# A fourth bank for the ring of exact scores, taken from the output of the heads

## What is computed

```python
x = ln(x + splat_attention(x))            # 16 heads of 16
x = ln(x + cross_attention(x, ctx))       # 16 heads of 16, 120 keys
x = ln(x + best_of_8_experts(x))
x = ln(x + causal_attention(x))           # 16 heads of 16
x = ln(x + two_blocks(x, ctx))            # self, then cross: 16 heads of 32, each with an MLP 256-1024-256
x = ln(x + four_of_16_experts(x))
# an attention, for every head:
p = exp(q @ k.T * scale - max)            # later divided by its row sum
o = p @ v                                 # v has a column of ones: the row sum comes along
```

## Time and profile before

| | us |
|---|---|
| median of 3 runs | 3960.23 |
| lowest, highest | 3958.79, 3975.51 |
| the profiled execution | 3954.29 |
| its span, first to last instruction | 3952.6 |
| PE busy | 3343.7 |
| DVE busy | 2807.9 |
| ACT busy | 2094.5 |
| POOL busy | 975.9 |

### The profile page before, as it was taken

One profiled execution on the slowest core, in us unless ns is written; L12 is line 12 of the kernel. 1 busy time (PEld: TensorE's weight loads), 2 busy tenths in 40 slices (PEclk: granted clock), 3 DMA queues, 4 the chain that ended last, 5 costly groups with the idle time before them and its releaser, 6 DMA issues. The chain is left out here.

```text
span 3952.6 us, 94629 instructions
## 1 busy us (share of the span) xinstructions
PE 3343.7 (85%) x38960; PEld 2374.8 (60%) x38960; DVE 2807.9 (71%) x6362; ACT 2094.5 (53%) x4222; POOL 975.9 (25%) x1808
## 2 busy tenths in 40 slices
PE   1889888989898888888988888899888898988886
PEld 1666565666565656656656656566655665655554
DVE  5777776777776767777776667677776677777664
ACT  4745565455556554564564555645555556455551
POOL 0312341122222321131132222212342112124310
PEclk9989888988898889888988988898988898989887
DMA  5000000000000000000000000000000000000000
GB/s 163 3 3 2 2 3 4 9 7 3 2 2 2 8 3 7 7 3 2 7 2 2 5 4 7 6 4 2 1 2 3 9 9 4 2 2 2 1 4 6
DMA packets 30365, 31.49 MB, mean 8 GB/s; under 512 B 8673, under 2 KB 26482, under 8 KB 29938
## 3 DMA queue, kind: packets, MB, share of 16 engines
q1 hardware_dynamic: 29938, 25.44, 2.1%
HBM read 21.24 MB, written 4.19 MB: 6 GB/s over the span
## 5 line engine op out<-in xcount | busy, mean ns | idle before, releaser
L1103 ACT ACTIVATE p<-bank,p_log 128x512 f32<-128x512 f32 (+2 forms) x1280 | 746.8, 583 | 1331.3 <-PE bank L797 1266.6
L1669 POOL TENSOR_TENSOR prob<-p,prob 120x256 f16<-120x256 f32 (+2 forms) x512 | 455.5, 890 | 1742.4 <-ACT prob L1104 1741.3
L1104 ACT ACTIVATE prob<-bank,p_log 128x512 f16<-128x512 f32 (+2 forms) x1280 | 747.3, 584 | 0.0
L1368 DVE TENSOR_REDUCE negm<-bank 128x2 f16<-128x512 f32 (+1 forms) x1280 | 675.3, 569 | 33.9 <-PE bank L752 18.2
L1286 DVE TENSOR_TENSOR prob<-p,prob 128x512 f16<-128x512 f32 (+2 forms) x768 | 474.0, 624 | 188.9 <-ACT prob L1104 178.8
L774 PE MATMUL bank<-q,k 32*128 32x256 f16 (+2 forms) x6144 | 496.8, 289 | 65.1 <-issue 34.7
L668 PE MATMUL bank<-w_exp,ident_h 128*128 128x512 f16 x1280 | 429.3, 421 | 32.3 <-DVE negm L1368 15.2
L1678 POOL TENSOR_SCALAR_AFFINE_SELECT probm<-prob 128x128 f16<-128x128 f16 x1024 | 325.9, 358 | 340.4 <-DVE prob L1286 340.4
L774 PEld LDWEIGHTS bank<-q,k 32*128 32x128 f16 (+1 forms) x6144 | 307.9, 110 | 142.7 <-issue 66.8
L797 PE MATMUL bank<-ident_h,negm 128*128 128x256 f16 (+2 forms) x2560 | 384.9, 273 | 0.0
L1661 POOL TENSOR_TENSOR rstd<-veps,minus_half 128x2 f32<-128x2 f32 (+1 forms) x208 | 149.7, 720 | 887.9 <-DVE veps L1261 887.3
(11 more groups left out here) (300 smaller groups left out, 6286.5 us busy)
## 6 DMA issues: line engine op xcount, KB each, us to landing
x<-in_x SPq DMA_DIRECT2D x16, 256.0 KB, 2.7
out<-z SPq DMA_DIRECT2D x16, 256.0 KB, 2.2
xa<-in_li SPq DMA_DIRECT2D x9, 256.0 KB, 4.6
x<-in_li SPq DMA_DIRECT2D x7, 256.0 KB, 4.3
z<-in_wq SPq DMA_DIRECT2D x4, 256.0 KB, 4.4
z<-in_li SPq DMA_DIRECT2D x4, 256.0 KB, 4.1
cx<-in_ctx_t SPq DMA_DIRECT2D x16, 60.0 KB, 1.8
cx<-in_ctx SPq DMA_DIRECT2D x16, 60.0 KB, 1.8
```

Of the source, the lines that this page charges most:

```text
L1103: act(p32[0:n, g % PBUF32, 0:cols], ps[0:n, 0:cols], ACT.Exp, bias=p_log[0:n, :], scale=a.scale)
L1104: act(prob[0:n, 0, g % PBUF, 0:cols], ps[0:n, 0:cols], ACT.Exp, bias=p_log[0:n, :], scale=a.scale).then_inc(a_done, one(a_done))
L1368: v.tensor_reduce(negm[:, h * NT:(h + 1) * NT], ring_v[bank_of(e, v_full)][:, :].rearrange("p (t n) -> p t n", t=NT)[:, :, 0:ATTNS[k].keys ...
L1669: g.tensor_tensor(prob[0:n, 1, m % PBUF, 0:cols], p32[0:n, m % PBUF32, 0:cols], prob[0:n, 0, m % PBUF, 0:cols], ALU.subtract).then_inc(pp_ ...
```

## The change

`RING` becomes three numbers: `ring_a` has four banks (0 to 3), `ring_v` three (4 to 6), `o_bank` one (7). A use of `ring_a` now waits for the use four before it. A group of heads waits for the normalisation of the group just before it, since both use bank 7.

```diff
-RING = 3
+RING_A, RING_V, RING_O = 4, 3, 1
...
-        ring_a, ring_v, o_bank = bank[0:3], bank[3:6], bank[6:8]
+        ring_a, ring_v, o_bank = bank[0:RING_A], bank[RING_A:RING_A + RING_V], bank[8 - RING_O:8]
...
                     taken = releases[which]
-                    if len(taken) >= RING:
-                        e.wait_ge(*taken[-RING])
+                    ring = ring_a if which == "a" else ring_v
+                    if len(taken) >= len(ring):
+                        e.wait_ge(*taken[-len(ring)])
...
-                    return (ring_a if which == "a" else ring_v)[(len(taken) - 1) % RING]
+                    return ring[(len(taken) - 1) % len(ring)]
...
                     group = sent(o_full)
-                    if h % a.group == 0 and group >= 2:
-                        e.wait_ge(o_done, group - 1)
+                    if h % a.group == 0 and group >= RING_O:
+                        e.wait_ge(o_done, group + 1 - RING_O)
...
-                        o = o_bank[group % 2][:, c:c + D + 1]
+                        o = o_bank[group % RING_O][:, c:c + D + 1]
...
-                    o = o_bank[(sent(o_done)) % 2][:, :].rearrange("p (t c) -> p t c", t=NT)[:, :, 0:n * (D + 1)]
+                    o = o_bank[sent(o_done) % RING_O][:, :].rearrange("p (t c) -> p t c", t=NT)[:, :, 0:n * (D + 1)]
```

More of the change, by code:

```diff
@@ L91, in __init__ @@
     def __init__(self):
-        self.increments, self.awaited = {}, {}
+        self.increments, self.awaited, self.ring = {}, {}, {}
     def one(self, sem):
@@ L109, in bank_of @@
     def bank_of(self, engine, full):
-        return (self.awaited[(str(engine.engine), full.num)] - 1) % RING
+        return (self.awaited[(str(engine.engine), full.num)] - 1) % self.ring[full.num]
 def heads_of(a):
@@ L386, in decoder @@
         counts = Counts()
+        counts.ring.update({a_full.num: RING_A, v_full.num: RING_V})
         one, sent, upcoming, bank_of = counts.one, counts.sent, counts.upcoming, counts.bank_of
@@ L631, in slot @@
                         ready[what] = taken[-1]
-                        low_banks.append((len(taken) - 1) % RING)
+                        low_banks.append((len(taken) - 1) % len(ring))
                         high[what] = high_ready, len(low_banks)
-                    return (ring_a if which == "a" else ring_v)[(len(taken) - 1) % RING]
+                    return ring[(len(taken) - 1) % len(ring)]
                 def to_raw(*what):
@@ L832, in weighted_values @@
                             for pp, vp in PARTS:
-                                last = mm(o_bank[group % 2][:, c:c + D], probm[:, pp, g % MBUF, i, :],
+                                last = mm(o_bank[group % RING_O][:, c:c + D], probm[:, pp, g % MBUF, i, :],
                                           val[s][:, vp, i * HEADS + h, 0:D], start=False,
```

## The result

The changed kernel takes 4025.59 us (median of 4 runs, 4021.61 to 4030.78), against 3961.95 us of the kernel before beside it. The ratio is 1.0155, 95% interval [1.0128, 1.0181]: it is slower by 1.6%. The forecast was 4100 us, 3.5% slower.

The account below looks back on a forecast made before the run. The prediction took PE to set the end, its idle time being what could move. From 3954.3 us, less 36 for the ring, plus 122 for new waits and 58 for the clock, it got 4098, named 4100; range 4042 to 4160.

Parts of the forecast that it names:

- What bounds the kernel: Whole kernel: PE sets the end, busy 3343.7 of 3952.6 us; its 609 us of idle time is what can move.
- The new wait: At PE's changes of head group: 158.5 us of waiting for DVE's normalisation, 118 inside pairs, 38 at heads 13 to 14.
- What of it reaches the end: Behind the 61 waiting places: 122 us comes through, nine tenths of that inside pairs, 37% at heads 13 to 14.
- the clock: PE's granted clock after idles above 2 us: 22 more low stretches at 2.6 us each cost 58 us.
- The ring's gain: At PE's waits for ring_a: a fourth bank gains 36 us, a little over half of five waits totalling 64.6 us.
- The signs named for the profile: Changed profile: o_tok waits 130 to 160 us, ring_a waits nearly gone, two others down 20 to 40, PE busy up 30 to 60.
- The ring wins: Rival, stages between attentions: ring_a waits vanish and the clock falls less, 3890 us; chance of faster 0.03.
- The banks do not bind: Rival, ring_a: the fourth bank gives nothing, since a pair takes two at once; 4134 us, no chance of its own.
- the waits are absorbed: Rival, PE's waits on DVE: a third of 158.5 us passes, 3971 us; chance 0.05 shared with no-change rival, partly absorbed 0.09.
- The clock costs more: Rival, PE's clock: each of 38 long waits starts a 10 us low stretch, 4178 us; chance above 4160 is 0.13.
- Rotation does not matter: Rival, o_bank: only DVE's emptying is exposed, 29 us of new waits, 3947 us; chance 0.05 shared with absorbed waits.

Follow-up runs that it names:

- the waits alone: Kernel before, banks unchanged, but each group of heads waits for the normalisation of the group just before it, as with one output bank: 4111.53 us, ratio 1.0361.
- even groups: Groups of 32-feature heads hold six heads, not seven: on the changed kernel 3887.60 us; on the kernel before 3969.17 us; with rings of 3, 3, 1 3983.41 us.
- the pairs' wait back: Changed kernel, but the exact scores of a pair again wait for the use of ring_a three before, as with three banks: 4086.38 us, ratio 1.0321.

## Why the prediction was wrong, point by point

**What bounds the kernel** held: DVE, ACT and POOL have the same busy time in every kernel above, within 2%, and the times went with PE's idle time and with how long its matmuls took.

**The new wait** held in place, number and length. Inside pairs: 32 waits, 118 us worked out, 115.0 measured with nothing else changed; all: 158.5 against 147.9 us. The first place, 3.5 us by the earlier trace rows, is 3.40 us with the waits alone:

```profile
459.07 0.24 PE L825 MATMUL bank<-zero_one,prob 128*128 128x33 f16 x2 [3.40 <-DVE o_tok L1395]
```

**What of it reaches the end, and the clock**, together 180 us: measured 143 by the ratio. In the profiled runs it was 155, of which 103 idle (I had 122) and 52 busy time (I had 58, for the clock). The steps were a little too large, by 25 to 37 us in all. The count behind the 58 held as well: idle times of PE above 2 us, the load at the start left out, are 70 in the trace of the kernel before and 94 with the waits alone, where I had counted 22 more, and the time at 1.2 GHz went from 830 to 1001 us, where 22 x 7.5 are 165. At 52 us for these 171 a microsecond at the low level cost 0.30. One reading in that step was wrong: the idle of 4.26 us in the earlier trace rows ends at 526.90, so it begins at 522.64, inside the first window of the earlier trace rows, and the clock fell at 525.30 while PE stood, not behind the idle. That the waits inside pairs pass nearly whole and the others little held too: 126 and 17 us, of waits of 115 and about 33.

**The ring's gain was the step that failed.** The sum had 36 us; the runs show 82 to 86 beside the new waits, and 96 to 100 with even groups. With 84 for 36 and nothing else changed the sum would have been 4050 us, inside the range; of the 73 us by which it was too high, about 48 are this term and 25 the two of the paragraph above. Two things in it were wrong.

The first is the list. The waits "that end with a read of `ring_a`" were picked by the releaser's name, which left out the 34.7 us under "issue" and 3.9 at L774 on L1360: 64.6 should have been about 103, and use by use it is 102.

The second is what the list is worth. I took a little over half of it as idle time and put the ring's effect on PE's busy time and clock at nothing in the sum, though a rival had it. Between the waits alone and the changed kernel, PE's idle time falls by 36 us (711.9 to 675.9) and its busy time by 47 (3395.7 to 3348.3). That the idle part equals my 36 is luck. Some 97 us of waits on the ring with the waits alone (34.7 + 21.3 + 13.6 + 9.7 in the rows above, and some smaller) become 8 or less, and PE's other waits grow by more than 50 us, those for the normalisation alone by 23.5 (147.9 to 171.4). The sum had no term for the 47 us. With groups of six the ring gives the same two parts, 46 us idle (622.5 to 576.1) and 47 busy (3351.4 to 3304.0).

What the 47 consist of stays open. The time at 1.2 GHz is 936 us for 1001, which by the 0.22 to 0.40 of the earlier trace rows is worth an estimated 14 to 26. Besides, some waits on the ring show no idle time: in the kernel before 115 uses of `ring_a` begin within 0.13 us of the read they wait for with no idle time of PE above 0.15 us before them, in the changed kernel 19. What PE lost at these was not parted.

The same place as above shows both sides at once in the changed kernel. PE's first exact scores and head 7:

```profile
448.71 0.28 PE L776 MATMUL bank<-q,k 32*128 32x256 f16 x2
...
456.48 0.24 PE L827 MATMUL bank<-zero_one,prob 128*128 128x33 f16 x2 [6.03 <-DVE o_tok L1397]
```

DVE's normalisation there:

```profile
455.79 0.62 DVE L1397 TENSOR_TENSOR o_tok<-bank,recip 128x448 f32<-128x448 f32 x1
```

The wait of 2.80 us ahead of the exact scores is gone, and head 7 waits 6.03 us in place of the 3.5 that I had worked out, because PE comes to it so much earlier. To compare executions, count from DVE's L1360 (now L1362) of this place, which begins at 455.09 in the kernel before. With the waits alone it is the first of these rows, in the changed kernel the second:

```profile
452.98 1.28 DVE L1360 SCALAR_TENSOR_TENSOR v<-bank,v 128x512 f16<-128x512 f32 x2
```

```profile
451.10 1.28 DVE L1362 SCALAR_TENSOR_TENSOR v<-bank,v 128x512 f16<-128x512 f32 x2
```

Head 7 begins 2.53 us behind it in the kernel before (457.62), 6.09 us with the waits alone (459.07) and 5.38 us in the changed kernel (456.48). PE reaches head 7 3.3 us earlier than with the waits alone, but begins it only 0.7 us earlier. I had sized the new wait with PE's arrival as it was; an earlier arrival makes the wait longer, not its end later. So the 171.4 us of waits in the changed kernel are no measure of their cost. The run with the pairs' wait back shows the same from the other side: its span (4082.7 us) is 58 us above that of the changed kernel; 50 of them are PE's busy time (3398.4 us) and only 8 idle.

**The signs named for the profile.** The waits on `o_tok` came, and those of the earlier trace rows all but vanished. PE's two other waits shrank by 20 us together, the least that I had named. The mean granted clock fell by one hundredth, not two, and PE's busy time rose by 4.6 us, not 30 to 60: the ring gave back most of what the new waits cost there.

**The rivals.** "The ring wins" was the nearest in mechanism: nearly all waits of the ring went and some of the low clock with them, but the gain was 82 to 86 us and not its 117, and the new waits were not small enough, as the rule for it said (about 1 us a change inside a pair; it was 3.6). With even groups there are none inside pairs, and the kernel is faster, 2%. "The banks do not bind" was false, "the waits are absorbed" true only of those between pairs. "The clock costs more" had 120 us for the clock; it was 52. "Rotation does not matter" fell for groups of seven: it exposes 29 us, and the second output bank was worth 143. With groups of six it was worth 14 to 23. The Trainium skill, Perfetto Trace Analysis, on matmuls, says that groups should rotate through different banks so that emptying overlaps. This case agrees, with 143 us at groups of seven and 14 to 23 at groups of six.

## What to carry to other kernels

A second output bank is worth the time by which the reader comes late, not the time that the reading takes: ask where the reading engine's instruction stands in its queue when the bank is full, and whether a group can end where other work lies between (here six heads in place of seven turned a change of banks from 1.6% slower to 2.0% faster). And before a gain is summed from a list of waits, take the waits under "issue" on lines that wait for the same resource into it, and test one of them in the timeline against the reader of that bank. Then give busy time a term of its own: here over half of the ring's gain came as busy time of the same matmuls.

## What was not expected of the hardware

A kernel freed of waits on a ring gets "less busy" too: 47 us fewer of PE's busy time with the same 38,960 matmuls, with groups of seven and again with groups of six. The clock accounts for an estimated 14 to 26 us of the first; the rest stays open, and the covered waits above are a candidate that no run tested. And fillers can pay in a wait: 256 extra matmuls, at least 55 us of work, made the kernel with the waits alone 27 us faster by ratio, at a granted clock of 0.891 for 0.878 in the profiled executions.
